# One chunk's rows fetched by SyncE in every fourth edge group, and three shifts of work around barrier 2

## What is computed

```python
xn = layernorm(x)
# graph attention, 8 heads of 32
h = xn @ W                                   # [N, 8, 32]
ea = leaky(s_src[src] + s_dst[dst], 0.2)     # per edge and head
ea = exp(ea - segment_max(ea, dst)[dst]); ea = ea / (segment_sum(ea, dst)[dst] + 1e-8)
gnn = segment_sum(h[src] * ea, dst)          # [N, 256]
# linear attention and an MLP of 768 hidden units, with its own layernorm
x = x + gnn + mix(xn)
# mixture of experts: the two best of 8, each 256 -> 512 -> 256, on layernorm(x)
x = x + sum over e of gate_e * (gelu(xf @ W1_e + b1_e) @ W2_e + b2_e)
```

## Time and profile before

| | us |
|---|---|
| median of 3 runs | 3238.33 (3231.4 to 3256.0) |
| the profiled execution | 3240.78 |
| its span, first to last instruction | 3239.5 |
| busy: PE, DVE, ACT, POOL | 2646.1, 2015.4, 1553.4, 2236.9 |

### The profile page before, as it was taken

The page is one execution under the profiler, slowest core; times in us unless marked ns, Lnnn a source line. Parts: engine busy times, 40 slices in busy tenths (PEclk is TensorE's granted clock), DMA queues, the critical chain, the costliest instruction groups (busy, mean ns, idle before and its releaser), DMA issues.

```text
span 3239.5 us, 42164 instructions
## 1 busy us (share of the span) xinstructions
PE 2646.1 (82%) x11525; PEld 2052.0 (63%) x11525; DVE 2015.4 (62%) x5482; ACT 1553.4 (48%) x3392; POOL 2236.9 (69%) x2187
## 2 busy tenths in 40 slices
PE   7657776888898888988899886564578999999998
PEld 6546555666675666656566564442357887878887
DVE  7445567667676777767677676787554555445422
ACT  5325544555554556545465454343344545445444
POOL 0277777777777777777777777777557766776644
PEclk9879988999999999989999898887789999999999
DMA  8797766566566666666656666556666666666663
GB/s 274 245 297 210 198 176 171 162 173 179 164 172 178 175 178 169 166 179 173 178 164 170 178 163 175 161 156 191 217 177 160 155 156 160 151 143 127 139 109 61
DMA packets 397718, 561.17 MB, mean 173 GB/s; under 512 B 71976, under 2 KB 318030, under 8 KB 397305
## 3 DMA queue, kind: packets, MB, share of 16 engines
q0 software_dynamic: 123696, 298.61, 36.3%
q1 hardware_dynamic: 196457, 170.61, 18.0%
q10 hardware_dynamic: 77255, 88.59, 9.9%
HBM read 402.43 MB, written 169.68 MB: 177 GB/s over the span
## 4 chain that ended last, share of the span: by engine, by line
PE 65%; DMA 10%; ACT 9%; issue 6%; DVE 5%; POOL 5%; ACTq 1%; SPq 0%; DVEq 0%; POOLq 0%
PE bank L1447 21%; PE bank L2494 10%; PE bank L2507 9%; PE bank L1179 7%; DMA rows<-table,srcix 7%; PE bank L1168 5%; POOL rows L1364 4%; PE bank L1141 2%; PE bank L684 1%; PE bank L685 1%; PE bank L949 1%; ACT L1488 1%; DMA last_d<-fout 1%; ACT L1284 1%; ACT e_hn L2085 1%
## 5 line engine op out<-in xcount | busy, mean ns | idle before, releaser
L1364 POOL DMA_INDIRECT rows<-table,srcix x1536 | 1476.4, 961 | 468.1 <-issue 333.4
L1447 PE MATMUL bank<-rows,onehot 128*128 128x272 f32 x3328 | 921.6, 424 | 56.3 <-ACT fout L1504 51.9
L1504 ACT ACTIVATE fout<-bank 128x272 f32<-128x272 f32 x1659 | 638.6, 397 | 589.1 <-PE bank L1447 541.9
L1447 PEld LDWEIGHTS bank<-rows,onehot 128*128 128x128 f32 x3328 | 661.3, 206 | 239.7 <-ACT fout L1504 77.9
L1601 DVE TENSOR_TENSOR rows<-rows,bank 128x1024 f32<-128x1024 f32 x416 | 483.7, 1212 | 171.8 <-ACT rows L1493 171.3
L2585 POOL DMA_INDIRECT out<-x_y,x_dest x203 | 326.3, 1607 | 244.1 <-DMA out<-x_y,x_dest 157.3
L2494 PE MATMUL bank<-x_int,x_w1c 128*128 128x256 f32 (+1 forms) x1696 | 380.5, 378 | 23.0 <-issue 19.7
L2507 PE MATMUL bank<-e_w,x_ht 128*128 x1624 | 373.9, 383 | 8.4 <-issue 6.2
L2494 PEld LDWEIGHTS bank<-x_int,x_w1c 128*128 128x128 f32 x1696 | 317.5, 195 | 74.2 <-issue 32.2
L2533 ACT ACTIVATE x_ht<-bank,x_b1c 128x256 f32<-128x256 f32 (+1 forms) x424 | 172.9, 462 | 392.1 <-PE bank L2494 391.9
L2507 PEld LDWEIGHTS bank<-e_w,x_ht 128*128 128x128 f32 x1624 | 302.8, 192 | 51.3 <-issue 13.8
(11 more groups left out here) (461 smaller groups left out, 3405.6 us busy)
## 6 DMA issues: line engine op xcount, KB each, us to landing
frag<-fout ACTq DMA_DIRECT2D x104, 544.0 KB
x_in<-sorted_d SPq DMA_DIRECT2D x97, 260.0 KB
rows<-table,srcix POOLq DMA_INDIRECT x1536
x_b2c<-in_L_ffn_b SPq DMA_DIRECT2D x106, 128.0 KB, 3.6
frag<-in_x ACTq DMA_DIRECT2D x1, 13416.0 KB
table<-hr SPq DMA_DIRECT2D x24, 544.0 KB, 4.0
xs<-in_x SPq DMA_DIRECT2D x24, 512.0 KB, 6.1
xg<-in_x SPq DMA_DIRECT2D x24, 512.0 KB, 6.0
```

The source lines that it names most:

```text
L1364: p.indirect_dma_start(out=B.rows[b][:, j, :], out_offset=None, in_=B.table[:, :], in_offset=bass.IndirectOffsetOnAxis(ap=chunk_columns(B. ...
L1447: pe.matmul(B.banks[2 + c % 3][:, 0:ROW], B.onehot[k % 2][:, j, :], B.rows[k % NR][:, j, :], start=True, stop=True).then_inc(S.sum, 1)
L1504: a.activation(B.fout[k % 2][:, j, :], B.banks[2 + c % 3][:, 0:ROW], ACT.Copy).then_inc(S.ev, 1)
```

## The change

1. SyncE fetches the last chunk of groups 26, 30, ... 94 (18 chunks), which GpSimd then leaves out. It loads the chunk's 128 ids into one partition, then into registers, 16 with each call, and issues one DMA of one row (1088 bytes) for each edge, 8 rows at each of 16 calls, that is 32 rows a group from group 21 on. At the last call it waits for all rows, loads the next ids, waits for the old sums of that place in the ring, and moves the 128 rows from the buffer `spare` into `rows` with one DMA (139 KB). `copy_scores` of these groups waits for the move. `spare` lies where `gram` lay, which the mix has finished with by then (the wait for `S.mixp`).
2. GpSimd does no `reach` at barrier 2, and `MEET` counts one engine less there (9 in place of 10).
3. The schedule's last point is 16 steps lower: round 1 ends at its rows, and its plan runs from `rest()`, behind the last group and before the last window's merge.
4. Behind barrier 2 ScalarE calls `fetch_nodes` for rounds 2 and 3. In `paces` the lead of rounds 2, 3, 4, 5 is 2, 5, 8, 11 places (2, 12, 12, 12 before); the later ones stay.
5. Two pairs of semaphores become one each (`ix_rows` in `ix_in`, `x_b` in `e_w`), with the counts fitted.

```diff
@@ schedule() @@
-            (FIRST_FROM + 4, first + routing)]
+            (FIRST_FROM + 4, first + routing - 16)]
@@ before edges_pool @@
+LOADS = 16
+SPARE_FROM, SPARE_EVERY = 20, 4
+SPARE_CALLS = 4 * SPARE_EVERY
+SPARE_GROUPS = list(range(SPARE_FROM + SPARE_EVERY + 2, SPLIT - 1, SPARE_EVERY))
+SPARE_CHUNK = CB - 1
+
+def spared_to(k, b):
+    return sum(g <= k and g % NR == b for g in SPARE_GROUPS)
+
+def spare_sync(sp, S, B):
+    def ids(i):
+        if i < len(SPARE_GROUPS):
+            c = SPARE_GROUPS[i] * CB + SPARE_CHUNK
+            sp.dma_start(B.spare_ids[:, :], B.src[c:c + 1, :]).then_inc(S.spare, 16)
+    sp.wait_ge(S.mixp, 5)
+    ids(0)
+    yield
+    for i, g in enumerate(SPARE_GROUPS):
+        rows = [0] + [P * (t + 1) // SPARE_CALLS for t in range(SPARE_CALLS)]
+        sp.wait_ge(S.spare, 16 * ((P + 1) * i + 1))
+        if i:
+            sp.wait_ge(S.moved, 16 * i)
+        at = {}
+        for lo, hi in zip(rows, rows[1:]):
+            for e in range(lo, hi):
+                if e % LOADS == 0:
+                    at = dict(enumerate(B.nc.values_load_multi_w_load_instructions(
+                        B.spare_ids[0:1, e:e + LOADS], engines=(mybir.EngineType.SP,), min_val=0, max_val=N_NODES,
+...
+                sp.dma_start(B.spare[e:e + 1, :], B.table[bass.ds(at[e], 1), :]).then_inc(S.spare, 16)
+            if hi == P:
+                sp.wait_ge(S.spare, 16 * (P + 1) * (i + 1))
+                ids(i + 1)
+                sp.wait_ge(S.sum, (g - NR) * CB + SPARE_CHUNK + 1)
+                sp.dma_start(B.rows[g % NR][:, SPARE_CHUNK, :], B.spare[:, :]).then_inc(S.moved, 16)
+            yield
@@ edges_pool() @@
+            if j == SPARE_CHUNK and k in SPARE_GROUPS:
+                continue
@@ edges_sync() @@
+    spare = spare_sync(sp, S, B)
...
         for _ in range(3):
             beside()
+            if k > SPARE_FROM:
+                next(spare, None)
...
         beside()
+        if k >= SPARE_FROM:
+            next(spare, None)
@@ copy_scores() @@
-        a.wait_ge(S.rows_in[r], 16 * (CB * (k // NR) + min(CB, REAL - k * CB)))
+        a.wait_ge(S.rows_in[r], 16 * (CB * (k // NR) + min(CB, REAL - k * CB) - spared_to(k, r)))
+        if k in SPARE_GROUPS:
+            a.wait_ge(S.moved, 16 * (SPARE_GROUPS.index(k) + 1))
@@ route_sync() @@
-        if r == FIRST_ROUNDS:
-            fetch_nodes(sp, S, B, r)
-            fetch_nodes(sp, S, B, r + 1)
@@ paces() @@
-    lead = lambda r: 2 if r == FIRST_ROUNDS else EARLY * (1 + (r == len(ROUNDS) - 1))
+    lead = lambda r: min(EARLY, 2 + 3 * (r - FIRST_ROUNDS)) * (1 + (r == len(ROUNDS) - 1))
@@ pool_program() @@
-    reach(p, S)
@@ scalar_program() @@
     barrier(a, S, 2)
+    for r in (FIRST_ROUNDS, FIRST_ROUNDS + 1):
+        fetch_nodes(a, S, B, r)
```

More of the change, by code:

```diff
@@ L156, in __init__ @@
         self.vec = new("vector_chain")
-        self.ix_in, self.ix_rows, self.ix_fl = new("ix_in"), new("ix_ends_out_in"), new("ix_first_last")
+        self.ix_in, self.ix_fl = new("ix_ids_then_ends_in"), new("ix_first_last")
         self.ix_tp, self.ix_cp, self.ix_num = new("ix_turned"), new("ix_copied"), new("ix_numbers")
@@ L173, in __init__ @@
         self.near, self.far = several("near_out", 2), several("far_out", 2)
+        self.spare, self.moved = new("spare_in"), new("spare_moved")
         (self.sce, self.tsc, self.flags, self.oh, self.inb, self.eav, self.fm, self.exp, self.tw, self.tail, self.wgh,
@@ L189, in __init__ @@
             "mg_alpha_spread", "mg_alpha_copied", "mg_run_done", "mg_run_turned", "mg_part_ready", "mg_summed"))
-        self.e_w, self.e_x, self.e_x1 = new("e_gate_in"), several("e_x_in", NF), several("e_x1_out", NF)
+        self.e_w, self.e_x, self.e_x1 = new("e_gate_then_biases_in"), several("e_x_in", NF), several("e_x1_out", NF)
         self.e_f, self.e_g = [several(f"e_frag_in{b}_", 2) for b in range(NF)], several("e_sorted_out", NH)
@@ L199, in __init__ @@
         self.free = new("early_free")
-        self.x_w1, self.x_w, self.x_b = new("x_first_weights_in"), new("x_second_weights_in"), new("x_biases_in")
+        self.x_w1, self.x_w = new("x_first_weights_in"), new("x_second_weights_in")
         self.x_in, self.x_y, self.x_wt = several("x_in", NI), several("x_out", NOUT), new("x_first_weights_copied")
@@ L205, in __init__ @@
             "x_turned", "x_in_copied", "x_fc1_done", "x_gelu_done", "x_fc2_done", "x_y_read_scaled", "x_aimed"))
-MEET = {1: 5, 2: 10}
+MEET = {1: 5, 2: 9}
 FREE = 4
@@ L323, in __init__ @@
     def __init__(self, nc, a, out):
+        self.nc = nc
         self.a, self.out = a, out
@@ L340, in __init__ @@
         self.gram = A("gram", [P, KD, D + 1], F32)
+        mark_gram, nc.sbuf_base = nc.sbuf_base, keep
+        self.spare, self.spare_ids = A("spare", [P, ROW], F32), A("spare_ids", [1, P], I32)
+        assert nc.sbuf_base <= mark_gram
+        nc.sbuf_base = mark_gram
         self.wqa, self.bqa = A("wqa", [P, KD, D], F32), A("bqa", [P, D], F32)
@@ L568, in index_vector @@
     w = B.wide[:, :]
-    v.wait_ge(S.ix_rows, 80)
+    v.wait_ge(S.ix_in, 112)
     v.tensor_tensor(B.span[:, :], B.dlb[0:1, :], B.dfb[0:1, :], ALU.subtract).then_inc(S.ix_hot, 1)
@@ L810, in heads @@
             sp.wait_ge(S.ix_cp, len(TURNS) + 1)
-            sp.dma_start(B.rows_d.rearrange("j (b c) -> (j b) c", c=P), B.flt[:, :]).then_inc(S.ix_rows, 16)
-            sp.wait_ge(S.ix_rows, 16)
+            sp.dma_start(B.rows_d.rearrange("j (b c) -> (j b) c", c=P), B.flt[:, :]).then_inc(S.ix_in, 16)
+            sp.wait_ge(S.ix_in, 48)
             for j, to in ((0, B.dfb), (1, B.dlb)):
-                sp.dma_start(to[:, :], B.rows_d[j].partition_broadcast(GH)).then_inc(S.ix_rows, 16)
+                sp.dma_start(to[:, :], B.rows_d[j].partition_broadcast(GH)).then_inc(S.ix_in, 16)
             for j, to, at in ((0, B.dfb_t, TAIL), (1, B.dlb_t, TAIL - 1)):
-                sp.dma_start(to[:, :], B.rows_d[j, at:CHUNKS].partition_broadcast(GH)).then_inc(S.ix_rows, 16)
+                sp.dma_start(to[:, :], B.rows_d[j, at:CHUNKS].partition_broadcast(GH)).then_inc(S.ix_in, 16)
     for k in range(NS):
@@ L1352, in first_fetches @@
             fetch_sums(p, S, B, r, i)
+LOADS = 16
[24 more added lines that the diff above has]
+                        B.spare_ids[0:1, e:e + LOADS], engines=(mybir.EngineType.SP,), min_val=0, max_val=N_NODES,
+                        skip_runtime_bounds_check_because="sources are node numbers, the pad's is N_NODES, and the table has N_PAD rows")[1], e))
+                sp.dma_start(B.spare[e:e + 1, :], B.table[bass.ds(at[e], 1), :]).then_inc(S.spare, 16)
[5 more added lines that the diff above has]
+            yield
 def edges_pool(p, S, B, groups):
@@ L1985, in sorted_rows, with fetch_nodes @@
     return x.rearrange("(p t) d -> p t d", t=SUB)
-def fetch_nodes(sp, S, B, r):
+def fetch_nodes(e, S, B, r):
     if r >= NF:
-        sp.wait_ge(S.e_x1[r % NF], stored_to(r - NF))
-        sp.wait_ge(S.e_hn, R_FIRST[r - NF] + R_TILES[r - NF])
+        e.wait_ge(S.e_x1[r % NF], stored_to(r - NF))
+        e.wait_ge(S.e_hn, R_FIRST[r - NF] + R_TILES[r - NF])
     for k in ROUNDS[r]:
@@ L1994, in fetch_nodes @@
         o = s - R_FIRST[r]
-        sp.dma_start(B.e_x[r % NF][:, o:o + n, :], rows_of(B.xm_d, s, n)).then_inc(S.e_x[r % NF], 16)
+        e.dma_start(B.e_x[r % NF][:, o:o + n, :], rows_of(B.xm_d, s, n)).then_inc(S.e_x[r % NF], 16)
 def first_sync(sp, S, B):
@@ L2464, in fetch @@
             sp.wait_ge(S.x_h, HT * (j - NW + 1))
-        sp.wait_ge(S.x_b, 16)
+        sp.wait_ge(S.e_w, 48)
         sp.dma_start(B.b1c[w][:, :], B.b1[:, bass.ds(ex, 1), :]).then_inc(S.x_wc[w], 16)
@@ L2678, in sync_program @@
     barrier(sp, S, 2)
-    sp.dma_start(B.b1[:, :, :], B.a["L0_ffn_b1"].rearrange("e (k p) -> p e k", p=P)).then_inc(S.x_b, 16)
+    sp.dma_start(B.b1[:, :, :], B.a["L0_ffn_b1"].rearrange("e (k p) -> p e k", p=P)).then_inc(S.e_w, 16)
     late(route_sync(sp, S, B, LATER), experts_sync(sp, S, B))
```

## The result

The changed kernel takes 3392.35 us (median of 4 runs, 3385.43 to 3395.75) against 3236.24 in the runs beside it: a ratio of 1.0463, 95% interval 1.0437 to 1.049. It is 156 us slower, and the forecast of 3208 was wrong in sign. Rival A, SyncE that can't keep up, came true.

The account below looks back on a forecast made before the run. GpSimd's gathers were taken to bound the edge stage, 1.25 us a chunk. Terms -21 - 0 - 3.4 - 6 = -30.4 us gave 3208 us from the median 3238.3; range 3194 to 3261, the forecast's own 3194 to 3222.

Parts of the forecast that it names:

- Rival A: Edge stage: SyncE can't keep up with the row fetches and score copies wait for the move; 3261 to 3675, chance 0.22.
- The gathers' bound, and what one saves: Edge stage: GpSimd's gathers set the pace, 1.25 us each; 18 fewer save 22.5 us while GpSimd stays the bound.
- SyncE's price of a row: SyncE's one-row DMAs in the edge stage: address, issue and load together 0.46 us a row, bounds 0.44 and 0.81.
- the point of decision: Edge stage: SyncE keeps up only if a row costs at most (78.75 - 16.5)/128 = 0.49 us.
- the upper end of the forecast's own range: Whole kernel: 3222 us, with part 4 at half and the move late.
- its middle case: SyncE in the edge stage: issue at 0.354 and a cheap load, 0.56 us a row, some 3377 us.
- Its form by registers: SyncE's loads: time goes by registers, 0.27 us each; 0.69 us a row with a cheap issue, 3675 us; chance 0.10.
- What a late move costs: Edge stage: the added waits of SyncE and of ScalarE's score copy cost 0 to +6 us, taken as +1.5.
- Part 2, the drain: GpSimd before barrier 2: the 6.0 us gap is saved but covered by its wait at the barrier: 0.
- Part 3, the plan: VectorE behind the last group: round 1's plan moves into the last merge's wait, -3.4 us, bounds -3.4 and 0.
- Part 4: Behind barrier 2: ScalarE's node loads -4 (bounds -6, 0) and shorter leads -2 (bounds -6, +5), together -6 us.
- The bound that I had named: Expert stage: SyncE already waits 101.9 us for sent rows; shorter leads add to that, leads at worst +5 us.

Follow-up runs that it names:

- run without spared chunks: Changed kernel with GpSimd gathering every chunk, parts 2 to 4 kept: 3248.3 us, ratio 1.0011; with the old leads as well: 3233.7 us, 0.999.
- fixed addresses: Changed kernel with the spared rows fetched from table rows 0 to 127, no register loads or address work on SyncE: 3227.9 us, ratio 0.9943.
- every fifth group with the old leads: Changed kernel with a spared chunk in every fifth group in place of every fourth, leads as before the change: 3218.6 us, ratio 0.9928.
- every sixth: Changed kernel with a spared chunk in every sixth group (12 chunks) and the leads as before the change: 3222.1 us, ratio 0.9946.
- every fifth group: Changed kernel with a spared chunk in every fifth group (15 chunks) in place of every fourth (18): 3228.4 us, ratio 0.9958.
- part 1 alone: Kernel before the change with only the spared chunks (and the merged semaphores) added: 3392.7 us, ratio 1.0454.
- The pairs above: Runs compared without spared chunks, then every fifth group: adding ScalarE's loads 1.0032 to 1.0011, 0.9951 to 0.9928; new leads 0.999 to 1.0011, 0.9928 to 0.9958.

## Why the prediction was wrong

**The gathers' bound, and what one saves: right.** 1.25 us a gather and room in the other engines. Where SyncE kept up, the time fell by about the price, by the ratios and each against its run without spared chunks: some 22 us for 18 chunks with fixed addresses (22.5 priced), 20 for 15 in every fifth group with the old leads (18.8), 14 for 12 in every sixth (15).

**SyncE's price of a row: the step that failed.** I put 0.46 us, in the range from 0.44 to 0.81, with 0.49 as the point of decision, and gave the margin 3.3 us in four groups. It measured 0.58, at most, in the cycle shown. By terms: the address was right, 0.416 - 0.225 = 0.19 (0.07 of it is the gap that fixed addresses have too). The issue of one row is 0.225 at the median, under what I took. The load I put at 0.02 a row, one call at one register's price: 1.248/16 = 0.08 at the median, and 13.9 us over 128 rows, 0.11, in the cycle. The medians alone, 0.19 + 0.225 + 0.08 = 0.49, stand exactly on the point. Of the 0.09 us above them some 0.03 are loads longer than their median (13.9 us against 8 x 1.248 = 10.0) and some 0.03 row fetches longer than theirs (46.7% are 41.2 us, against 128 x (0.225 + 0.037 + 0.029) = 37.2): issues of up to 1.8 us and loads of up to 3.7, which a sum of shortest durations doesn't hold. The rest are gaps, those at the flag's branch among them. So the loads moved the price to the edge, and the tails pushed it over. The 14 us that are left of the cycle were 16.5 in the forecast.

One sum of the prediction doesn't come out: the upper end of the forecast's own range, 3222. By its terms a late move (-16.5), the plan (-3.4) and half of part 4 (-3) make 3215. The measured time is far outside either.

Rival A had the place and the mechanism, and its middle case, 0.56 us a row and 3377, came near in time, but by luck: it had a dear issue and a cheap load. Its form by registers was half right: sixteen registers cost more than four, at 0.057 us for each more, and my price of one register for sixteen was far too cheap, but one and four cost nearly the same. The Trainium skill, "Runtime: NRT & Kernel Launch", section "Instruction fetch mechanics", gives about 200 ns a register even in bulk. The trace doesn't agree: 1.248 us for sixteen are 0.08 each.

**What a late move costs: wrong.** I put 0 to +6 on the added waits. With SyncE as the bound the lateness is carried from one spared chunk to the next, so the ring covers it once and not each time. The run with fixed addresses, where SyncE kept up, shows how much of it arrives: there the moves run from 701.6 to 2074.7, 80.8 us apart, and the last gather starts at 2261.62. With the register work the last move comes 164.9 us later and the last gather 164.7, so all of it reaches the gathers. With the row's price under the point it is hidden: in every fifth group the point is (98.75 - 19.5)/128 = 0.62 us.

**Part 2, the drain: right, as far as the trace shows.** The gap is gone, and GpSimd still stands 17.4 us at the barrier (18.4 before), so nothing on the path waited for it; no run changed the drain alone. GpSimd at the end of the edge stage:

```profile
2426.27 1.01 POOL L1416 DMA_INDIRECT rows<-table,srcix_tail  x1 [0.30 <-issue]
2427.59 1.00 POOL L2006 DMA_INDIRECT sorted_d<-e_hn,e_row  x1 [0.30 <-issue]
...
2486.05 0.99 POOL L1991 DMA_INDIRECT e_fr<-frag,nodeix  x1 [17.42 <-SPq L216]
```

**Part 3, the plan: right.** The plan runs in the hole of the last merge, and VectorE waits there 1.02 us in place of 4.06:

```profile
2468.97 0.16 DVE L2347 CAST pl_ci<-pl_count 128x8 int32<-128x8 f32 x1
...
2472.27 0.16 DVE L2391 SCALAR_TENSOR_TENSOR pl_tile_row<-pl_num,pl_at 1x9 int32<-1x9 f32 x1
...
2474.59 0.23 DVE L1862 COPY mgp_mL<-bank 8x80 f32<-8x80 f32 x1 [1.02 <-PE bank L1750]
```

From the last gather to barrier 2 it is 2485.85 - 2426.27 = 59.6 us, against 2345.28 - 2279.92 = 65.4; 3.4 were forecast. In the runs with this part the stretch was 59.6 to 63.0, in that of part 1 alone, which lacks it, 66.4; no run changed the plan alone.

**Part 4: the loads right in sign and wrong in place, the leads wrong in sign.** ScalarE issues the four loads at the barrier, as said. What I overlooked is that VectorE has the first tiles' destinations ahead of round 2 in its order. Behind barrier 2, SyncE, ScalarE, TensorE and VectorE:

```profile
2485.85 0.39 SPq L2736 DMA_DIRECT2D x_b<-in_L_ffn_b  x1
...
2485.81 2.74 ACTq L2054 DMA_DIRECT2D e_x<-xm_d  x4
...
2500.82 1.09 PE L2539 MATMUL bank<-ident,x_in 128*128 128x128 f32 x4 [21.23 <-DMA x_in<-sorted_d]
...
2520.60 1.09 PE L2095 MATMUL bank<-ident,e_hn 128*128 128x128 f32 x8 [1.08 <-ACT e_hn L2141]
...
2500.81 0.17 DVE L2606 CAST x_dest<-x_in 128x2 int32<-128x2 f32 x1 [20.29 <-DMA x_in<-sorted_d]
...
2505.47 0.34 DVE L2606 CAST x_dest<-x_in 128x2 int32<-128x2 f32 x1 [4.16 <-DMA x_in<-sorted_d]
```

The first tile reaches TensorE 15.0 us behind the barrier, where it was 5.7. In the kernel before:

```profile
2350.98 1.09 PE L2483 MATMUL bank<-ident,x_in 128*128 128x128 f32 x4 [12.11 <-DMA x_in<-sorted_d]
```

That the nodes' loads do this shows in the run with them back on SyncE (total, times, longest):

```profile
PE bank L2542 <- DMA x_in<-sorted_d: 17.3, 5, 12.1
```

The longest wait is 12.1 us again. Whether the tile's rows stand behind the loads in a queue or share the DMA engines with them was not tried. VectorE stands 20.3 us before that tile's destinations and takes the second tile's (2505.47) before it begins round 2. So round 2's rows come to TensorE 34.8 us behind the barrier, 32.9 before: the stall that was to vanish moved to the tile. The pairs above give the loads a gain all the same, some 7 us (4 forecast, 6 at most): round 3 starts at TensorE 80 us behind the barrier in place of 83, and 81 in place of 86 in every fifth group. The leads were to bring 2 us, with +5 as the worst: by the pairs they cost 7 to 10, and what the traces show for it is the tiles that SyncE fetches later. The bound that I had named, its wait for sent rows, was the term, and I gave it too little. Why the loss shows more at the end of the expert stage than where TensorE waits is open: from barrier 2 to the end it took 894.2 us in the profile before and 907.1 with part 1 alone, with the same code behind the barrier, and 894.8 in every fifth group with the old leads and 902.4 in every sixth, again with the same code there, so that single profiles don't carry it.

**The sum.** -21, 0, -3.4 and -6 were forecast; +147 (part 1 alone, 1.0454), and nothing that can be told from 0 for the rest.

## What to carry to other kernels

Work that is given to an engine with idle time must be priced by rate: so many issues in a period, at mean durations with their tails, against a budget. Here the sum of medians stood exactly on the budget, the tails made the overrun, it came back every period, and the buffer covered it only once. A load of many registers must be priced as such and not as a load of one, so gathering rows by registers is paid twice, in the load and in the address. Before loads are moved ahead, look which engine's order has the displaced transfer's user first.

## What the runs showed that I had not expected

- A load of registers into SyncE took 0.28 us for one, 0.56 for four and 1.25 for sixteen (medians), and single ones up to 3.7. Among row fetches the load of one took 0.54.
- A DMA of one row of 1088 bytes was issued in 0.225 us at the median, but rows with a fixed address stood 0.295 us apart and rows with a register's address 0.416.
- A period too short by a tenth (78.75 us for some 88) cost 156 us, and 20 us more for it gave 12 of gain.
